# Layers 0 and 3 of an eight-stage transformer kernel: the order of splits, constants, value products, turned sums and gathered rows

## The reference, cut to what matters

```python
scores = einsum('bhnqd,bhnkd->bhnqk', qb, k2) * scale   # k2: the block before and the own one
scores = where(mask, scores, -1e30)
out = einsum('bhnqk,bhnkd->bhnqd', softmax(scores), v2)
```

## Time and profile before

| | us |
|---|---|
| median of 3 runs | 3271.84 (3271.39 to 3273.11) |
| the profiled execution: its own time | 3289.43 |
| its span | 3287.7 |
| TensorE busy in it | 3021.8 (92%) |
| VectorE, ScalarE, GpSimd busy | 1850.8, 1345.5, 312.7 |
| mean granted TensorE clock | 0.959 |

### The profile page before, as it was taken

One profiled execution on the slowest core, in us unless ns is written; L12 is line 12 of the kernel. 1 busy time (PEld: TensorE's weight loads), 2 busy tenths in 40 slices (PEclk: granted clock), 3 DMA queues, 4 the chain that ended last, 5 costly groups with the idle time before them and its releaser, 6 DMA issues.

```text
span 3287.7 us, 51279 instructions
## 1 busy us (share of the span) xinstructions
PE 3021.8 (92%) x14822; PEld 1861.3 (57%) x14855; DVE 1850.8 (56%) x4512; ACT 1345.5 (41%) x1937; POOL 312.7 (10%) x349
## 2 busy tenths in 40 slices
PE   4999999999989999999989999999998699999998
PEld 2455545554545555555545555556665467666666
DVE  5656565656647777777647767652223544445552
ACT  1634454445425555555543334322232233333433
POOL 0000000000000000000011111121111211111110
PEclk7999999999989999999989999999999799999999
DMA  8433543354221222222240111112212333333330
GB/s 262 123 99 102 154 129 102 98 157 132 63 72 51 55 60 61 55 59 55 72 176 32 51 38 38 45 56 74 97 62 64 88 91 91 91 85 91 85 86 20
DMA packets 135546, 281.34 MB, mean 86 GB/s; under 512 B 20176, under 2 KB 77904, under 8 KB 123440
## 3 DMA queue, kind: packets, MB, share of 16 engines
q1 hardware_dynamic: 122896, 241.75, 26.3%
q0 software_dynamic: 10464, 28.59, 3.0%
q10 hardware_dynamic: 2128, 10.30, 0.9%
HBM read 180.88 MB, written 104.40 MB: 87 GB/s over the span
## 4 chain that ended last, share of the span: by engine, by line
PE 77%; DVE 6%; ACT 6%; issue 5%; DMA 4%; SPq 1%; POOL 0%; ACTq 0%; DVEq 0%; another core or an unknown queue 0%; POOLq 0%
PE bank L483 9%; PE bank_u L545 7%; PE pair L529 7%; PE bank L506 5%; PE pair L585 5%; PE pair L686 3%; PE pair L1887 3%; PE pair L2708 3%; PE bank_m L2672 3%; PE pair L730 3%; PE bank L2672 3%; DVE nmax L859 2%; PE bank_m L483 2%; PE pair L494 2%; PE bank_m L506 2%
## 5 line engine op out<-in xcount | busy, mean ns | idle before, releaser
L762 ACT ACTIVATE probs<-pair 128x1024 f32<-128x1024 f32 x512 | 504.8, 1021 | 249.5 <-PE pair L529 246.0
L859 DVE TENSOR_REDUCE nmax<-bank 128x1 f32<-128x512 f32 x664 | 440.6, 684 | 215.3 <-PE bank L506 211.7
L859 DVE TENSOR_REDUCE nmax<-bank_m 128x1 f32<-128x512 f32 x360 | 246.1, 684 | 85.5 <-PE bank_m L506 78.3
L545 PE MATMUL bank_u<-probs,vext 128*32 128x512 f32 x2048 | 282.6, 625 | 0.3 <-ACT uraw L749 0.3
L2011 DVE CUSTOM_DVE_ANT_0 bank<-bank,mask_q 128x128 f32<-128x128 f32 (+1 forms) x320 | 118.5, 417 | 172.4 <-PE bank L1790 163.8
L529 PE MATMUL pair<-q_a,k_a 98*128 98x512 f32 x512 | 170.8, 442 | 32.0 <-DVEq L914 14.3
L506 PE MATMUL bank<-k_a,q_a 96*128 96x512 f32 x336 | 172.7, 549 | 21.1 <-DMA k_a<-parts_dram 17.8
L529 PE MATMUL pair<-q,k 98*128 98x512 f32 x512 | 167.4, 410 | 2.5 <-DVEq L1521 2.2
L506 PE MATMUL bank<-k,q 96*128 96x512 f32 x328 | 150.0, 491 | 17.7 <-DMA k<-parts_dram 10.5
L529 PEld LDWEIGHTS pair<-q_a,k_a 98*128 98x128 f32 x512 | 89.4, 198 | 124.0 <-ACT probs L762 67.0
L1922 ACT ACTIVATE probs<-pair 128x896 f32<-128x896 f32 x128 | 114.8, 915 | 76.5 <-PE pair L1808 71.1
(11 more groups left out here) (380 smaller groups left out, 5774.7 us busy)
## 6 DMA issues: line engine op xcount, KB each, us to landing
parts_dram<-parts SPq DMA_DIRECT2D x64, 512.0 KB, 2.9
q_a<-parts_dram SPq DMA_DIRECT2D x32, 512.0 KB, 5.2
k_a<-parts_dram SPq DMA_DIRECT2D x32, 512.0 KB, 7.0
q<-parts_dram SPq DMA_DIRECT2D x64, 256.0 KB, 3.7
xl<-xs SPq DMA_DIRECT2D x31, 512.0 KB, 4.4
xres<-xs SPq DMA_DIRECT2D x24, 512.0 KB, 3.9
xs<-xres SPq DMA_DIRECT2D x24, 512.0 KB, 3.0
x_in<-xg SPq DMA_DIRECT2D x74, 128.0 KB, 2.0
```

Of the source, the lines that this page charges most:

```text
L545: ins = nc.tensor.matmul(bank_u[32 * h:32 * h + 32, :], vext[:, kt, kv(g, h), :], probs[:, kt % 2, h * SEQ:(h + 1) * SEQ], start=(kt == 0) ...
L762: nc.scalar.activation(probs[:, kt % 2, hp * 2 * SEQ:hp * 2 * SEQ + n], st.tile(l, name)[:, 0:n], ACT.Exp).then_inc(st.free["act"].sem, 1)
L859: nc.vector.tensor_reduce(nmax[:, g % 2, qt, h:h + 1], sc.tile(l, name)[:], AX, ALU.max, negate=True).then_inc(sc.free["dve"].sem, 1)
```

## The change

Layer 0: the splits come in the order Q0, Q1, K0, K1, J0, J1, KN0, KN1, so JJ is read by splits 4 and 5 and freed behind split 5. At the start `ident` has a semaphore of its own, TensorE waits for it alone, and the memset of `k_a` goes behind the products that the projections need. In PRE0 and PRE3 SyncE waits for stack 0 to land before it issues stack 1. Layer 3: T2 and M1 stand ahead of V; S (3,6) and S (3,7) and DT0 stand between T and the projections; H4 to H7 come together, then `weigh(1)`, E (2,h), DT1, E (3,h); ScalarE's copy of sums 1 goes behind its first exponential of group 2. The gather goes token block by token block with a semaphore for each of four blocks, and VectorE adds a block's two rows as it lands, with a wait behind each add.

```diff
-SPLITS0 = ["Q0", "Q1", "K0", "K1", "KN0", "KN1", "J0", "J1"]
+SPLITS0 = ["Q0", "Q1", "K0", "K1", "J0", "J1", "KN0", "KN1"]
@@ sc_plan3
-                     + hs(2) + s3_uses(3)[4:6] + hs(3) + s3_uses(3)[6:]),
+                     + hs(2) + s3_uses(3)[4:6] + hs(3) + s3_uses(3)[6:] + turn_uses(0)),
-                    ("back", m_use(3) + hs(4, 5) + turn_uses(0) + hs(6, 7) + turn_uses(1)),
+                    ("back", m_use(3) + hs(4, 5, 6, 7) + turn_uses(1)),
@@ st_plan3
-("back", [("V", "dve"), ("T2", "act")] + e3_uses(0) + e3_uses(1))
+("back", [("T2", "act"), ("V", "dve")] + e3_uses(0) + e3_uses(1))
@@ act0
                     if i < 6:
-                        act.wait_ge(*high_ready.at(l, it, i - 1))
+                        act.wait_ge(*st.filled(l, it, "JJ"))
                     else:
-                        act.wait_ge(*st.filled(l, it, "JJ"))
+                        act.wait_ge(*high_ready.at(l, it, i - 3))
@@ dve0, low
-                if i in (1, 3, 7):
+                if i in (1, 3, 5):
                     dve.wait_ge(*split.at(l, it, i + 1))
                     dve.sem_inc(st.free["dve"].sem, 1)
@@ sp0, and the same in sp3
                 stack(0)
+                if not back:
+                    sp.wait_ge(*stack_ready(l, it, 0))
                 stack(1)
@@ pe3
             if back:
-                pe_values(pe, l, it, wv3)
-                pe_max_rows(pe, l, it, 1)
                 ...
                 ins.then_inc(st.full.sem, 1)
+                pe_max_rows(pe, l, it, 1)
+                pe_values(pe, l, it, wv3)
                 ...
                     hidden(i)
-                    maxima(3, 2 * i, 2 * i + 2)
+                    if i < 3:
+                        maxima(3, 2 * i, 2 * i + 2)
                 ...
                 pe_transpose_xn(pe, l, it)
             if back:
-                weigh(1)
+                maxima(3, 6, 8)
+                pe_turn_sums(pe, l, it, 0)
                 ...
                 pe_max_rows(pe, l, it, 3)
-                hidden(4)
-                hidden(5)
-                pe_turn_sums(pe, l, it, 0)
-                hidden(6)
-                hidden(7)
+                for i in range(4, 8):
+                    hidden(i)
+                weigh(1)
+                for h in range(GH):
+                    scores_t(2, h)
                 pe_turn_sums(pe, l, it, 1)
@@ act3
-                act_max_rows(act, l, it, 1)          # now behind the two hT activations
                 ...
-                act_copy_sums(act, l, it, 1)
                 for i in range(4, 8):
                     hidden(i)
                 for h in range(GH):
                     weights(2, h)
+                    if h == 0:
+                        act_copy_sums(act, l, it, 1)
@@ pool_gather_rows
-            for n in range(2 * TT):
-                ... .then_inc(rows_gathered.sem, 16)
+            for t in range(TT):
+                for n in (t, TT + t):
+                    ... .then_inc(rows_gathered[t].sem, 16)
@@ dve_combine
-            dve.wait_ge(*rows_gathered.at(l, it, 128 if l == COMB else 0))
             ...
-            for j in range(2):
-                for t in range(TT):
-                    n = j * TT + t
+            for t in range(TT):
+                dve.wait_ge(*rows_gathered[t].at(l, it, 32 if l == COMB else 0))
+                fence(dve)
+                for n in (t, TT + t):
                     step.mark(nc.vector.scalar_tensor_tensor(...))
-                step.wait()
+                    step.wait()
@@ dve3
                 maxima(3, 4, 8)
+                dve_normalise_heads(dve, l, it, step, 0)   # was behind the four low parts
@@ start
+            sp.dma_start(ident[:], d["ident"]).then_inc(ident_loaded, 16)
@@ vector, start: memset of k_a from second place to last, dve_setup 7 becomes 6 in the waits
-            nc.vector.memset(k_a[96:98, :, :, :], 1.0).then_inc(dve_setup, 1)
             ...
+            nc.vector.memset(k_a[96:98, :, :, :], 1.0).then_inc(dve_setup, 1)
@@ tensor, start
-            pe.wait_ge(consts, N0)
+            pe.wait_ge(ident_loaded, 16)
```

More of the change, by code:

```diff
@@ L255, in st_plan3 @@
 def st_plan3(front, back):
-    return parts_of(front, back, ("back", [("V", "dve"), ("T2", "act")] + e3_uses(0) + e3_uses(1)), ("front", [("T", "act")]),
+    return parts_of(front, back, ("back", [("T2", "act"), ("V", "dve")] + e3_uses(0) + e3_uses(1)), ("front", [("T", "act")]),
                     ("back", unused(0) + e3_uses(2) + e3_uses(3) + [("OT", "act"), ("OUT", "dve")]))
@@ L376, in build @@
         N0B = 16 * 8
-        dve_setup = sem("dve_setup")
+        dve_setup, ident_loaded = sem("dve_setup"), sem("ident_loaded")
         pool_setup = sem("pool_setup")
@@ L398, in build @@
         indices_ready = sig("indices_ready", [0, 0, 0, {PRE3: 1, MAIN3: 1}, {COMB: 1}], "gpsimd")
-        rows_gathered = Signal(sem("rows_gathered"), spread([0, 0, 0, {PRE3: 128, MAIN3: 128}, {COMB: 128}]), 0)
+        rows_gathered = [Signal(sem(f"rows_gathered{t}"), spread([0, 0, 0, {PRE3: 32, MAIN3: 32}, {COMB: 32}]), 0) for t in range(TT)]
         def fence(eng):
@@ L555, in raw0 @@
         def raw0(l, i):
-            if i in (4, 5):
-                return kn32[:, i - 4, :]
-            return st.tile(l, "JJ" if i > 5 else f"QK{i // 2}")[:, i % 2 * SEQ:(i % 2 + 1) * SEQ]
+            if i > 5:
+                return kn32[:, i - 6, :]
+            return st.tile(l, "JJ" if i > 3 else f"QK{i // 2}")[:, i % 2 * SEQ:(i % 2 + 1) * SEQ]
         def pe0(pe, l, it):
@@ L617, in pe0 @@
                 if not back:
-                    pe.wait_ge(dve_setup, 7)
+                    pe.wait_ge(dve_setup, 6)
                 claim("QK0")
@@ L1864, in pe3 @@
                 pe_max_rows(pe, l, it, 3)
-                hidden(4)
-                hidden(5)
-                pe_turn_sums(pe, l, it, 0)
-                hidden(6)
-                hidden(7)
+                for i in range(4, 8):
[3 more added lines that the diff above has]
+                    scores_t(2, h)
                 pe_turn_sums(pe, l, it, 1)
-            for h in range(GH):
-                if back:
-                    scores_t(2, h)
             for h in range(GH):
@@ L1931, in act3 @@
                 ins.then_inc(st.free["act"].sem, 1)
+                act_max_rows(act, l, it, 1)
                 for g in range(2):
@@ L1976, in pool_gather_rows @@
             fence(pool)
-            for n in range(2 * TT):
-                nc.gpsimd.indirect_dma_start(gathered[:, n, :], None, yg_dram[:, :],
-                                             bass.IndirectOffsetOnAxis(ap=ycur[:, n:n + 1], axis=0))\
-                  .then_inc(rows_gathered.sem, 16)
+            for t in range(TT):
+                for n in (t, TT + t):
+                    nc.gpsimd.indirect_dma_start(gathered[:, n, :], None, yg_dram[:, :],
+                                                 bass.IndirectOffsetOnAxis(ap=ycur[:, n:n + 1], axis=0))\
+                      .then_inc(rows_gathered[t].sem, 16)
         def dve_combine(dve, l, it, step):
             dve.wait_ge(*x_loaded.at(l, it, 16))
-            fence(dve)
-            dve.wait_ge(*rows_gathered.at(l, it, 128 if l == COMB else 0))
             fence(dve)
@@ L2043, in dve3 @@
                     dve.sem_inc(sc.free["dve"].sem, 1)
-            if back:
-                dve_normalise_heads(dve, l, it, step, 0)
             if front:
@@ L2777, in dve_first_rows @@
             step.end()
-        loads0 = [(ident, d["ident"]), (wq0, d["wq0"]), (wk0, d["wk0"]), (bq0, d["bq0"]), (bk0, d["bk0"]), (j_rows, d["j0"]),
+        loads0 = [(wq0, d["wq0"]), (wk0, d["wk0"]), (bq0, d["bq0"]), (bk0, d["bk0"]), (j_rows, d["j0"]),
                   (same_head, d["same_head"]), (lam, bc("lam0", 1)), (lscale, bc("scale0", 1))]
@@ L2834, in _ @@
             nc.gpsimd.memset(vext[:, :, :, HD:32], 1.0).then_inc(pool_setup, 1)
-            pool.wait_ge(dve_setup, 7)
+            pool.wait_ge(dve_setup, 6)
             pool0(pool, PRE0, 0, step)
@@ L2870, in _ @@
             act.dma_start(xs[BATCH * LAYERS, :, :], d["x"][0]).then_inc(xs_copied, 16)
-            act.wait_ge(dve_setup, 7)
+            act.wait_ge(dve_setup, 6)
             act0(act, PRE0, 0, step)
@@ L2916, in _ @@
             nc.vector.tensor_scalar(same_head[:], same_head[:], lam[:, 0:1], None, ALU.mult).then_inc(dve_setup, 1)
-            dve.wait_ge(dve_setup, 5)
+            dve.wait_ge(dve_setup, 4)
             for k in range(KT):
@@ L2955, in _ @@
             pe.wait_ge(pool_setup, 3)
+            pe.wait_ge(dve_setup, 7)
             with pe.Fori(0, BATCH - 1) as it:
```

1 line of the change is left out of this document (added).

## The result

The changed kernel takes 3295.49 us, median of 5 runs (3291.15 to 3302.22), beside 3271.84 for the kernel before (3267.07 to 3277.10): 1.0076 times, interval 1.0058 to 1.0094. It is 23.7 us slower where 23.5 less was forecast.

The account below looks back on a forecast made before the run. TensorE, busy 92% of the span, or what it waits for, was taken as the bound. Terms 3.9 + 4.9 + 2.5 + 1.9 + 9.8 + 0.5 = 23.5 off 3271.84 gave 3248.3 us, range 3238 to 3258.

Parts of the forecast that it names:

- the third rival: MAIN3, group 2: late tile completions while gather and stacks run grow to reach E (2,0), E (2,1); 3287 us, chance 0.08.
- PRE0 forecast 3.9: PRE0: 3.0 us from the earlier xnT copy at the start plus 0.9 from stack 0 landing sooner.
- the start: PRE0: moving the k_a memset last brings the xnT copy 6.9 us sooner; 3.0 kept, bounds 1.5 and 6.9.
- MAIN0 4.9: MAIN0: JJ freed sooner lets the second exponential follow at once; 0.7 us a round, 4.9 in seven.
- its clock 2.5: MAIN0: shorter idle time means fewer falls of the granted clock; 2.5 us, bounds -3 and 8.
- the first rival: MAIN0 and MAIN3: exponentials bind, gains are given back, only PRE0 and PRE3 pay; 3266 us, chance 0.09.
- COMB and PRE3 1.9: COMB adds by block gain 2.6 us; later stack 1 and M1 ahead of V cost 0.3 and 0.4; bounds 0 and 3.
- The fourth rival: PRE0 and PRE3: stack 1 lands 2 us late and is needed at once, costing 4 us; 3252, chance 0.10.
- MAIN3 1.4 a round: MAIN3: 0.9 at the start plus 0.6 in the middle less 0.1 for adds; 9.8 us in all.
- its sign of being wrong: MAIN3: wrong if rounds are not at least 0.7 us shorter in the mean, or a new wait exceeds 1 us.
- T2 first: MAIN3 round start: T2 ahead of V removes the hT wait, V's copies release the second E tile sooner; 0.9 us.
- the middle: MAIN3 round middle: moved `weigh(1)` covers idle time before the third E tile; 0.6 us a round taken.

Follow-up runs that it names:

- e3_before: Profile of the kernel before the change, unchanged, from a comparison in which no matmul semaphore came late: 3239.56 us.
- e4_after: The changed kernel once more, beside the kernel before, with no late semaphores: 3234.03 us, 0.9976 times.
- quiet comparisons: Comparisons, each alternating its kernels with the kernel before on one chip, in which no matmul semaphores came late.
- the second comparison: Against the kernel before (3287.34 us): the changed kernel again, 3308.86, 1.0068; the kernel before without MAIN3's row gathers, 3252.94, 0.9893.
- e7_gather2: Changed kernel with MAIN3's row gathers held until stack 2 has landed, against the kernel before: 3278.20 beside 3265.29 us, 1.0047.

## Why the prediction was wrong

**The step that failed** is the chance and the reason of the third rival: "Against it: group and gather keep their distance within 0.3 us. Chance 0.08." Two things in it were wrong. The late spell was read as something that E tiles meet; I didn't ask what else the edit moved into it. `weigh(1)` stood 14 us ahead of the gather (2716.92, gather at 2731.16) and was put 1.8 us behind it, where ScalarE's copy of sums and the next value products wait for its semaphore. And the distance was not kept. By the order alone, where nothing is late, E (2,0) moves from 2.6 us behind the first gather (e3_before) to 3.5 (e4_after), 0.9 and not 0.3. In the recorded trace `weigh(1)`, now inside the spell, is itself held up, from 2722.09 to 2725.6, and pushes E (2,0) to 5.2 us behind the gather (4.5 to 5.9 over the rounds), past the 4 us that the rival named as its point. That the rival's 3287 came near the measured 3295.5 is in part luck: it set 38 us of loss against 23.5 of gain, and the runs show 7.0 of gain, which leaves 30.7 for the loss.

In quiet comparisons (e3_before and e4_after) layer 3 from its first projection to the end is 7.7 us shorter (687.7 and 680.0), in the recorded one 17.9 longer: the late semaphores are worth 25.6 us of layer 3 in the changed kernel beyond what they already cost before (by the second comparison some 34 us of the kernel before). That the gathers make them late is shown by two experiments, one without the gathers and one with the gathers moved. That `weigh(1)`'s place carries the added loss is seen in the traces alone; the kernel with the middle put back met only quiet comparisons, so it is not shown by experiment, and the rival that T2 ahead of V brings the loss by moving the gather stands untested.

The other terms, by quiet comparisons where nothing else is said:

- PRE0 forecast 3.9: over all traces the first values come at 74.9 with layer 0's edits (14 traces, 73.6 to 77.2) and at 76.4 without (6, 75.2 to 77.7), 1.5. Stack 0 is issued 1.0 us sooner in the mean, less than the low bound of the start (1.5), and is first used 8.5 us behind its issue in place of 9.1, 0.5 and not 0.9. The start's term was mis-sized: in the recorded traces TensorE starts its projections 7.5 us sooner and waits 5.2 longer for stack 0. The stores take 6.3 to 6.7 us to land there in place of 3.1, and ScalarE waits 5.9 us for the first slot to be free, behind the same full DMA engines that the forecast named.
- MAIN0 4.9 and its clock 2.5: 765.2 us over the 11 quiet traces with the edits (763.6 to 767.5), 764.4 over the 4 without (763.3 to 765.1). Step wrong: "Gain 0.7 a round". The 0.7 is there (0.77) while the exponentials pace TensorE and ends at stack 0, which I had not looked at as the next one late. The clock gave nothing, and its sum was wrong too: 6.5 us at half clock cost 3.3 us a round, not 1.6. For MAIN0 this is the first rival's result by another mechanism.
- COMB and PRE3 1.9: COMB's 2.4 came in all traces with the edit (2.6 forecast). The fourth rival's mechanism did show in PRE3, without its price. These are the first products with stack 1 and the next ones behind, in the kernel before (e3_before, first projection at 2550.1) and the changed one (e4_after, 2548.2):

```profile
2576.39 1.22 PE L1790 MATMUL bank<-k,q 96*128 96x128 f32 x4 [0.20 <-DMA k<-parts_dram]
2580.31 1.56 PE L1790 MATMUL bank<-k,q 96*128 96x128 f32 x4
```

```profile
2576.41 1.22 PE L1792 MATMUL bank<-k,q 96*128 96x128 f32 x4 [2.63 <-DMA k<-parts_dram]
2578.19 1.56 PE L1792 MATMUL bank<-k,q 96*128 96x128 f32 x4
```

All traces with layer 3's edits have this wait, of 2.2 to 4.2 us; without them it is at most 0.4. Counted from the first projection, stack 1 is used 1.9 us later (26.3 and 28.2), but the products behind it stand at 30.2 and 30.0: TensorE idled there before, and makes the delay good. In PRE0 no wait for stack 1 appears in any trace, so the rival's 4 us did not come.

- MAIN3 1.4 a round: 0.6 (81.9 and 81.3), under the 0.7 that the forecast named as its sign of being wrong. TensorE's idle time falls by 1.1 (4.0 to 2.9 in the two windows above); the hT wait goes, V's copies leave 0.2, the third E tile waits no more and Q0 waits 0.3, much as forecast. 0.5 of it comes back as longer busy time, which is modelled; in these rounds the hidden products take 13.5 us in place of 12.6, the maxima 12.2 in place of 12.7. With the middle put back rounds are 81.4 to 81.5: T2 first is worth 0.4 to 0.5 and not 0.9, the middle 0.1 to 0.2 and not 0.6.
- Rounds are counted from V to V, and T2 and M1 now stand ahead of V, so PRE3, the first MAIN3 round and POST3 (0.5 forecast) can only be read together: 196.2 us in e3_before, 192.2 in e4_after. Most of these 4 us is clock: the first MAIN3 round has a mean granted clock of 0.957 in one and 0.998 in the other. No step named this, and it is not steady. PRE3 and the first round take 119.8 to 121.8 us in the three quiet traces without layer 3's edits, 118.4 to 120.5 in the seven with all of them.

So even without the spell the forecast was three times too large: 7.0 us measured, 23.5 forecast. I summed gains at single waits, where the next releaser (stack 0, exponentials, split maxima) stands close behind.

## What to carry to other kernels

When an edit moves work beside an indirect DMA, look in the trace of before for semaphores that come late behind such DMAs, and list everything that the edit brings into that stretch, value products and their copies too. Follow an early start to the end of the loop: the landing that doesn't move is what sets the round. Where two comparisons of an unchanged kernel differ by 1%, compare the kernels in both conditions; the sign of a change can depend on it.

## What the runs showed of the hardware

The same program had two conditions, 3241 to 3244 us (five comparisons) and 3265 to 3287 us (three), each steady within its comparison and both seen on one chip. In the slower one the semaphores of matmuls that end 2.4 to 11 us behind the first of a row of indirect DMAs come late, most of them 1 to 7 us (twice over 9, at the end of MAIN2). They are held to a moment and not for a length: in the changed kernel's MAIN3 rounds all come 11.4 to 11.7 us behind the first gather, whenever their matmul ended, in MAIN2 most come near 4.6 or 8.5 us or between 10 and 12. This is so in MAIN2 (33 to 40 of them over 1 us), PRE3 (up to 5) and MAIN3 (4 to 21), and nowhere in layers 0 and 1, which have no indirect DMAs. In the fifteen traces of the faster condition no semaphore of a matmul is over 0.1 us late. Leaving the indirect DMAs out of MAIN3 gives rounds of 81.8 us at full clock even in the slower condition, where the recorded trace of the kernel before has 86.3 to 90.1. Other loads need not be in flight: in e7_gather2 the gathers' own packets, 37.5% of the DMA engines' time, are enough. Why the condition comes and goes, and what delays the semaphore, stays open: what differs between the comparisons isn't in the traces.
